# Gated cross-attention, layer 0: the first pass of the software pipeline, its stages in another order on each engine

## What is computed

```python
ln_out = _ln(hidden_states, ln_w, ln_b)
q  = _ln(_fp8_linear(ln_out, wq,  ...))      # 16 heads of 128
qx = _ln(_fp8_linear(ln_out, wqx, ...))
k  = _ln(_fp8_linear(ln_out, wk,  ...))      # 8 groups
v  =     _fp8_linear(ln_out, wv,  ...)
core = _gqa(q, k, v)                          # softmax over the 256 own tokens
kx, vx = split(cond @ w_kv_x.T)
xout = _gqa(qx, _ln(kx), vx)                  # softmax over the 1601 context rows
catq = _div_clamp_fp8(concatenate([core, xout]), proj_smooth)
out  = (catq @ wproj.T) * (proj_in_scale * proj_w_scale)
```

## Time and profile before

| | us |
|---|---|
| median of 3 runs | 1722.6 (1717.89 to 1725.0) |
| the profiled execution | 1721.58 |
| its span | 1719.8 |
| PE busy / DVE busy / ACT busy / POOL busy | 1616.0 / 1393.7 / 1381.0 / 1273.5 |

### The profile page before, as it was taken

The page is one execution under the profiler, slowest core; times in us unless marked ns, Lnnn a source line. Parts: engine busy times, 40 slices in busy tenths (PEclk is TensorE's granted clock), DMA queues, the critical chain, the costliest instruction groups (busy, mean ns, idle before and its releaser), DMA issues. The chain is left out here.

```text
span 1719.8 us, 43340 instructions
## 1 busy us (share of the span) xinstructions
PE 1616.0 (94%) x16022; PEld 1011.1 (59%) x16022; DVE 1393.7 (81%) x3487; ACT 1381.0 (80%) x2317; POOL 1273.5 (74%) x1170
## 2 busy tenths in 40 slices
PE   3799999999999999999999999988998999999997
PEld 1466777767776677767777777766553333333332
DVE  8889999999999989999888888889995755555422
ACT  4688888788888788888888888873337999999996
POOL 3558778787787877887877787765896989989400
PEclk9899999999999999999999999998999999999998
DMA  4299989999999999999989999996323232222100
GB/s 175 87 177 203 195 206 205 195 205 222 202 189 200 190 198 185 224 211 207 196 194 218 217 194 209 211 186 175 104 44 108 44 77 39 44 39 45 26 14 14
DMA packets 608867, 261.07 MB, mean 152 GB/s; under 512 B 576528, under 2 KB 581648, under 8 KB 607248
## 3 DMA queue, kind: packets, MB, share of 16 engines
q1 hardware_dynamic: 604432, 258.05, 70.3%
q10 hardware_dynamic: 4224, 0.25, 0.2%
HBM read 99.15 MB, written 17.29 MB: 68 GB/s over the span
## 5 line engine op out<-in xcount | busy, mean ns | idle before, releaser
L1750 PE MATMUL pv<-PT,VV 128*128 128x256 bf16 (+1 forms) x2880 | 340.6, 275 | 12.1 <-DMA PT<-PB 12.1
L1730 PE MATMUL score<-KK,QT 128*128 128x512 bf16 (+2 forms) x1920 | 341.5, 322 | 6.5 <-DVE mxp L1225 6.5
L2316 POOL TENSOR_TENSOR l_rr<-l_rr,mhalf 128x32 f32<-128x32 f32 (+1 forms) x60 | 333.2, 5553 | 5.0
L1490 ACT ACTIVATE PB<-S,rsum 128x1024 bf16<-128x1024 f32 (+1 forms) x256 | 246.5, 988 | 106.0 <-DVE rsum L1256 81.6
L1750 PEld LDWEIGHTS pv<-PT,VV 128*128 128x128 bf16 (+1 forms) x2880 | 280.7, 99 | 79.9 <-issue 31.8
L1247 DVE SCALAR_TENSOR_TENSOR PB<-S,rsum,PB 128x1024 bf16<-128x1024 f32 (+1 forms) x256 | 297.6, 1163 | 3.1 <-ACT PB L1490 3.1
L1730 PEld LDWEIGHTS score<-KK,QT 128*128 128x128 bf16 x1920 | 158.1, 98 | 144.0 <-DVE mxp L1225 12.6
L1480 ACT ACTIVATE S<-S,nmx 128x1601 f32<-128x1601 f32 x128 | 210.2, 1643 | 7.2 <-DVE nmx L1237 7.0
L2582 ACT ACTIVATE P<-score 128x1024 f32<-128x1024 f32 x196 | 199.1, 1060 | 12.6 <-PE score L2674 5.9
L1068 POOL TENSOR_SCALAR S<-S,rsum 128x256 f32<-128x256 f32 x128 | 73.1, 571 | 129.8 <-DVE rsum L1256 116.2
L2694 PE MATMUL pv<-P,V 128*9 128x256 f32 (+1 forms) x2288 | 154.2, 384 | 3.8 <-DVE pv L2120 2.4
(11 more groups left out here) (264 smaller groups left out, 3577.6 us busy)
## 6 DMA issues: line engine op xcount, KB each, us to landing
x<-rs_d SPq DMA_DIRECT2D x16, 936.0 KB, 5.3
rsb<-rs_d SPq DMA_DIRECT2D x16, 936.0 KB, 5.5
wsb<-w_split SPq DMA_DIRECT2D x46, 256.0 KB, 4.7
wsb<-w_split SPq DMA_DIRECT2D x23, 512.0 KB, 4.9
wpr<-in_wprojT SPq DMA_DIRECT2D x23, 512.0 KB, 6.5
context_d<-stage SPq DMA_DIRECT2D x16, 400.2 KB, 3.7
l_ctx<-context_d SPq DMA_DIRECT2D x4, 1601.0 KB, 7.2
rawh<-in_w_all SPq DMA_DIRECT2D x12, 512.0 KB, 5.5
```

The source lines that it names most:

```text
L1490: e.activation(m.PB[n % 2][:, 2 * a:a + b], m.S32[n % 2][:, a:b], ACT.Copy, scale=m.rsum[n % 2][:, 1:2]).then_inc(s["p_hi"], 1)
L1730: i = e.matmul(m.score[:, at:at + b - a], qt[:, kind, qp, q * P:(q + 1) * P], kk[:, kp, a:b], start=(k == 0), stop=(k == 2))
L1750: i = e.matmul(m.pv[:, at:at + 256], vv[0:rows, v, t, :], m.PT[k % 2][0:rows, turned(c, a), :], start=(c == first and r == 0), stop=(c == ...
L2316: e.tensor_tensor(rr, rr, m.mhalf[0:rows, 0:NH1], ALU.pow).then_inc(s["l1_rr"], 1)
```

## The change

The pass `it == -1` is taken out of the shared loop body of DVE, ACT and POOL and written out by itself (`first()`, on POOL an `if` with `continue`); PE and SP keep the loop with single moves. The stages are the same but for these: `pool_round_end` is gone, so that roundings 4 to 6 end on DVE; roundings 6 and 7 and the low part of group 1's last weights (`dve_weights_low(1, 3)`) go from the first pass to iteration 0; the store of group 1's split weights goes behind the row of key scales, to the head of iteration 0 on SP; ACT's and POOL's waits for `xq_done` 8 are gone; PE does `scores(0, 0)` ahead of iteration 1's first queries, with a wait for `xw_done` (the score bank also holds the turned tokens); the padding memsets go to POOL's prologue.

```diff
@@ pool_prologue
+    for i in range(2):
+        e.memset(m.S32[i][:, SC:SELFC], 0.0).then_inc(s["p_pad"], 1)
...
-    pool_both_norms(e, m, s, 1, TB, NT)
@@ dve_prologue
     dve_round(e, m, s, 0)
     dve_context_low(e, m, s, 0, 0)
-    dve_round(e, m, s, 1)
     dve_context_low(e, m, s, 0, 1)
-    dve_weights_low(e, m, s, 0, 2)
...
-    dve_round(e, m, s, 2)
-    dve_weights_low(e, m, s, 0, 3)
@@ act_prologue
     act_weights_high(e, m, s, 0, 0)
+    act_scaled_inputs(e, m, s, 0)
     act_weights_high(e, m, s, 0, 1)
-    act_scaled_inputs(e, m, s, 0)
     act_context_high(e, m, s, 0, 0)
+    act_context_high(e, m, s, 0, 1)
     act_scaled_inputs(e, m, s, 1)
-    act_context_high(e, m, s, 0, 1)
@@ sp_attention
-        if it == -1:
+        if it == 0:
             sp_store_weights(e, m, s, 1)
-        if it == 0:
             sp_small(e, m, s)
@@ pool_attention
-        if it == 0:
-            e.wait_ge(s["xq_done"], 8)
...
+        if it == -1:
+            query_norm(0, 0)
+            query_low(0, 0)
+            pool_both_norms(e, m, s, 1, TB, NT)
+            query_norm(0, 1)
+            key_norm(0)
+            pool_context_low(e, m, s, 1, 0)
+            pool_context_low(e, m, s, 1, 1)
+            query_low(0, 1)
+            pool_split_weights(e, m, s, 1, 0)
+            pool_split_weights(e, m, s, 1, 1)
+            continue
@@ dve_attention
+    def first():
+        query_stats(0, 0)
+        dve_weights_low(e, m, s, 0, 2)
+        keys_low(0, 0)
+        dve_round(e, m, s, 1)
+        keys_low(0, 1)
+        dve_round(e, m, s, 2)
+        dve_weights_low(e, m, s, 0, 3)
+        keys_low(0, 2)
+        e.wait_ge(s["x_rest"], 16)
+        dve_statistics(e, m, s, 1, m.x, TB, NT)
+        keys_low(0, 3)
+        query_stats(0, 1)
+        dve_normalise(e, m, s, 1, m.x, m.xn, TB, NT)
+        dve_round(e, m, s, 3)
...
+        values_low(0, 0)
+        dve_sum_weights(e, m, s, 1)
+        dve_centre_weights(e, m, s, 1)
+        dve_context_low(e, m, s, 1, 0)
+        values_low(0, 1)
+        dve_context_low(e, m, s, 1, 1)
+        dve_weights_low(e, m, s, 1, 0)
+        dve_norm_weighted(e, m, s, 1, 0)
+        dve_norm_weighted(e, m, s, 1, 1)
+        values_low(0, 2)
+        dve_round(e, m, s, 4)
+        dve_weights_low(e, m, s, 1, 1)
+        values_low(0, 3)
+        dve_round(e, m, s, 5)
+        dve_weights_low(e, m, s, 1, 2)
...
@@ in the loop, behind keys_low(it + 1, 1)
+        if it == 0:
+            dve_round(e, m, s, 6)
@@ behind invert(4 * it)
+        if it == 0:
+            dve_weights_low(e, m, s, 1, 3)
@@ behind query_stats(it + 1, 1)
+        if it == 0:
+            dve_round(e, m, s, 7)
@@ act_attention
+    def first():
+        keys_high(0, 0)
+        query_norm(0, 0)
+        keys_high(0, 1)
+        query_full(0, 0)
+        keys_high(0, 2)
+        keys_high(0, 3)
+        sums_out(0)
+        query_norm(0, 1)
+        act_context_high(e, m, s, 1, 0)
+        values_high(0, 0)
+        act_context_high(e, m, s, 1, 1)
+        values_high(0, 1)
+        act_weights_high(e, m, s, 1, 0)
+        query_full(0, 1)
+        act_scaled_inputs(e, m, s, 4)
+        values_high(0, 2)
+        act_weights_high(e, m, s, 1, 1)
+        act_scaled_inputs(e, m, s, 5)
+        values_high(0, 3)
...
         if it == 0:
             e.wait_ge(s["p_pad"], 3)
-            e.wait_ge(s["w_lo_dve"], 16)
-            e.wait_ge(s["w_lo_pool"], 8)
...
-            e.wait_ge(s["xq_done"], 8)
+            e.wait_ge(s["w_lo_dve"], 8)
+            e.wait_ge(s["w_lo_pool"], 4)
@@ pe_attention
+        if it == 0:
+            scores(0, 0)
         queries(it + 1, 0)
-        scores(4 * it, 0)
+        if it > 0:
+            scores(4 * it, 0)
...
-        if it == -1:
-            pe_turn_normed(e, m, s, 1)
...
         turn_queries(it + 1, 1)
+        if it == -1:
+            pe_turn_normed(e, m, s, 1)
         values(it + 1, 2)
```

95 lines of the change are left out of this document (20 added, 75 removed).

## The result

The changed kernel took **1724.68 us** (median of 20 runs, 1717.64 to 1729.04), the kernel before 1720.02 beside it (20 runs): a ratio of **1.0026**, interval 1.0016 to 1.0036. Over all three the mean is 1723.9 us for 43 runs and 1721.1 for 90 runs of before: **2.8 us slower**, where 2.3 us faster were forecast. That lies within 0.5% and in the range given; the sign is wrong. (The 1720.3 us forecast was reckoned from a median of three runs, 1722.6, which 20 runs put at 1720.0; so the differences are compared here, not the times.)

A forecast was written before the change was run, and what follows sets the result against it. DVE's queue was taken to bound the path to iteration 1: 66.48 + 2.07 + 11.9 - 2.1 = 78.35 against 80.63, so 2.3 us earlier, 1720.3 us from a median of 1722.6; range 1714.5 to 1725.

The forecast's parts named there:

- The five waits: DVE waiting for other engines in the first pass and at iteration 0's head: 1.3, 2.0, 0.9, 1.45 and 1.4 us.
- the sum over DVE's queue: DVE's work plus waits up to tile 0's second `p_lo` in iteration 0: 78.35 against 80.63, 2.3 us earlier.
- The stretching: DVE operations slowed while POOL is mid-operation, 4.7 us over the roundings before; 2.6 would remain, 2.1 us less.
- the 0.9, 1.2 and 0.5 said: Slowing left on DVE: rounding 0's end beside POOL's context, rounding 2 beside `query_low(0, 0)`, and `p_lo` beside `query_low(1, 0)`.
- what it moves there is moved at the end: PE is saturated from some 98 us to layer 0's attention end, so a shifted start shifts the end equally.
- the distance from there to the end unchanged: Expected in the new profile: iteration 1's queries near 95.4, and the time from them to the end as before.
- something later in the attention that a shift in time sets off: A loss past 8.6 us arising in the attention after the first pass; chance 0.03.
- The path of the transposes: From 80.63 to 97.68: transposes of P, their landing and one `times_v`, none of it changed.
- A: First pass: ACT and POOL run further ahead, DVE's waits vanish; 7.2 us earlier, 1715.4 us; chance 0.19.
- B: POOL's `key_norm` holds rounding 3 on DVE for 2.65 us; 0.4 us later, 1723.0 us, or 1725.1; chance 0.10.
- C: SP's later weight store delays the transposes if DVE's last weights come after 74; about 1723 us; chance 0.03.
- D: Gain lost behind 80.63, tile 1's transposes held by the weight load between; no change, 1722.6 us; chance 0.05.

The follow-up runs named there:

- its variants: Changed kernel with PE's first scores again behind iteration 1's first queries: 1.0006; with roundings 6 and 7 and group 1's last weights back in the first pass: 1.0009.
- before with the store late: Kernel before with only SP's store of group 1's split weights moved to the head of iteration 0: 0.9993.
- The guard: Changed kernel plus a wait in iteration 1 that keeps POOL's magnitudes behind DVE's last low parts of group 2's weights: 1.0006.
- the forced order on the kernel before: Kernel before plus a wait in iteration 1: DVE makes group 2's last low parts only after POOL has taken pair 0's magnitudes: 1.0022, 1725.04 us.
- the pair run side by side: Kernel before and changed kernel, both with waits putting POOL behind DVE in iteration 1 and at token roundings, and POOL's token splitting later: 0.9986 and 0.9997.

## Why the prediction was wrong

**The five waits were right**: 7.37 us for 7.05, each within 0.4.

**The first step that failed: the sum over DVE's queue, 2.38 us too low** (78.35 against 80.73). It failed in the step "4.85 + 1.3 + 2.0 + 0.9 + 1.45 + 1.4 = 11.9 us ... I find no further wait". Measured idle time is 13.75 us: 4.94 at the start, 7.37 in the five waits, and 1.44 in gaps of 0.04 us or less between instructions, some forty of them. Those were in the 14.15 us of before too, and I rebuilt the idle time from named waits alone while taking the work from windows that leave the gaps out. The same sum made for the kernel before would have come out short as well: its 14.15 us hold 1.3 us of such gaps. The rest is 0.53 of work (66.98 against 66.48 + 2.07 - 2.1 = 66.45), 0.32 in the waits and 0.09 at the start: 1.44 + 0.53 + 0.32 + 0.09 = 2.38 (4.94 for the 4.85 of the prediction). So of 2.3 us of gain the gaps alone took 1.4.

**The stretching** moved more than it went. The roundings lost theirs much as forecast, and the three places where some was left measured 0.96, 0.91 and 0.25 us for the 0.9, 1.2 and 0.5 said: in the groups that answer to the earlier trace rows, the first operation takes 282 ns instead of 526, the third 300 instead of 445:

```profile
L631 DVE TENSOR_SCALAR stage<-stage 128x512 bf16<-128x512 bf16 x8 | 2.3, 282 | 0.0
L637 DVE TENSOR_SCALAR ex<-ex 128x512 int16<-128x512 int16 x8 | 2.4, 300 | 0.3
```

That is 3.1 us, of which the second of the five operations took 0.6 back (407 ns for 332). But the centring of the weights (2.53 us instead of 1.52) came to lie beside POOL instead, and the low parts of the context kept their one stretched operation of 2.22 us (mean of four 1489 ns, before 1468), now ahead of the first keys: 1.0 of the 1.5 us by which these came later than forecast (20.16 for 18.7). I placed the operations that I took relief for, and not those that were then moved into their place. (Alone, a rounding's first operation took 0.28 us in most rows, not the 0.23 that the prediction reckons with.)

**The second step that failed: "what it moves there is moved at the end", and "the distance from there to the end unchanged".** With a start 1.59 us earlier the distance grew by 7.0 in the profiled execution: 5.1 between the starts of iterations 1 and 30, of it 4.0 in PE's waits, and 1.9 behind. The two further profiles of the changed kernel had waits of 16.6 and 16.1 (its variants 15.8 and 17.6), and the mean of the three is 17.5 against 15.5 for before and before with the store late: 2 us, with a wide scatter. The stretch is bound by PE for most iterations and not in iteration 2, where DVE and POOL meet within a few tenths of a microsecond; the order turned there, DVE's pair took 1.55 us longer, PE waited 2.8 us instead of 1.6 (2.8 to 2.9 in all five profiles), and in four of the five its clock fell behind that wait. The guard takes it away (37.3 to 37.4 us instead of 38.2 to 40.2) and the forced order on the kernel before brings the wait back (3.05 us, ratio 1.0022); that is the part of the loss that is shown. What iteration 19 lost in the first profile did not come back in the others. I had this at 0.03, as "something later in the attention that a shift in time sets off", with a threshold of 8.6 us that hid the smaller and likelier size. It should have had a place of its own and a row of the trace: operations of DVE that stand within half a microsecond of a long one of POOL.

**The path of the transposes** held in the one profile: 80.77 to `times_v` at 93.47 is 12.7 us, before 80.66 to 93.72, 13.1. Over all profiles it ranged over 1.9 us (11.2 to 13.1 from the end of `p_lo`), so it isn't the constant that the prediction took it for. What came behind, the clock in `times_v`, was taken as fixed at the low value that the profile of before happened to show.

**The rivals.** A didn't come: the waits stayed. B was rightly doubted for `key_norm` (0.34 and 0.69 us beside it), and the mechanism it named was at work elsewhere, in iteration 1. C: the store went out at 71.79 instead of 68, ahead of the transposes by 9 us; the run with the store alone gave 0.9993. D is nearest: no gain, but because there was none at 80.73 to lose; whether one would have been lost behind it stays open.

**Open**: the 1.9 us behind the start of iteration 30 in the first profile (617.9 us against 616.0; the other two profiles of the changed kernel had 615.8 and 614.8, so it is likely scatter), why the clock in iteration 6 falls with the guard and not without; and whether the new first pass costs something of itself, up to the 2 us by which the pair run side by side differs.

## What to carry to other kernels

When a sum is made from busy time and named waits, put the gaps between instructions in, or check that the same sum gives the time of the kernel before. Before a shift in time is called neutral for what comes behind, list the places where VectorE and GpSimd meet within half a microsecond or so of each other: there the order can turn. A wait on a semaphore that puts the engine on the path first settled it here in iteration 2, though the whole gained too little from it to be told apart. Take several profiles before a place is blamed: the largest loss of the first pair, 3.4 us in iteration 19, was half that or less in the two further profiles of the changed kernel, and gone in one. And where a GpSimd operation of 3 us starts just ahead of a VectorE operation that TensorE waits for, look there before tidying the first pass: moving one such operation gave 2.2 us by the ratio.
